# Cross attention and value experts in one block, with the first tiles of x1 normalised beside the last batch

## The reference

```
x = x + tanh(g_xattn) * cross_attention(layernorm(x), ctx)     # 16 heads of 16
x = x + tanh(g_ffn) * switchhead(layernorm(x))                 # 8 heads of 128
# switchhead(x), 8 value experts and 8 output experts for each head, top 2 of each:
gate_v, gate_o = top2(sigmoid(x @ sel_v.T)), top2(sigmoid(x @ sel_o.T))   # normalised
q, k = x @ q_w.T, x @ k_w.T
v    = sum_e gate_v[e] * (x @ v_w[e])
out  = sum_e gate_o[e] * softmax(q k.T / sqrt(128)) v @ o_w[e]
```

## Time and profile before

| | us |
|---|---|
| median of 3 runs | 1936.9 (1934.24 to 1937.22) |
| the profiled execution, by the clock of the runs | 1935.28 |
| its span in the profile | 1933.5 |
| TensorE busy | 1873.0 (97%) |
| VectorE busy | 1503.0 (78%) |
| ScalarE busy | 1137.4 (59%) |
| GpSimd busy | 935.6 (48%) |

### The profile page before, as it was taken

One profiled execution on the slowest core, in us unless ns is written; L12 is line 12 of the kernel. 1 busy time (PEld: TensorE's weight loads), 2 busy tenths in 40 slices (PEclk: granted clock), 3 DMA queues, 4 the chain that ended last, 5 costly groups with the idle time before them and its releaser, 6 DMA issues. The chain is left out here.

```text
span 1933.5 us, 57514 instructions
## 1 busy us (share of the span) xinstructions
PE 1873.0 (97%) x13454; PEld 1145.7 (59%) x13454; DVE 1503.0 (78%) x4285; ACT 1137.4 (59%) x3588; POOL 935.6 (48%) x1368
## 2 busy tenths in 40 slices
PE   5999999999997999999999999999999999999998
PEld 2678888888875555444444445545555555555553
DVE  6688888899887962555555556668999999999989
ACT  3678888888886444444444445545555555555543
POOL 4122222222212011666666666665776676776767
PEclk9999999999998999999999999999999999999999
DMA  3777888888871585000000023122222222222201
GB/s 124 144 117 118 119 120 120 119 119 120 119 98 55 214 330 208 27 27 20 21 27 27 27 67 105 55 66 72 71 80 66 80 74 70 80 67 79 75 13 66
DMA packets 192148, 174.22 MB, mean 90 GB/s; under 512 B 51921, under 2 KB 183378, under 8 KB 190034
## 3 DMA queue, kind: packets, MB, share of 16 engines
q1 hardware_dynamic: 189906, 165.06, 37.7%
q0 software_dynamic: 2176, 8.39, 1.2%
HBM read 112.41 MB, written 60.98 MB: 90 GB/s over the span
## 5 line engine op out<-in xcount | busy, mean ns | idle before, releaser
L1475 POOL TENSOR_TENSOR o_side<-o_side,o_tmp 128x256 f32 (+1 forms) x528 | 397.8, 753 | 194.7 <-POOL o_side L1475 72.3
L1244 PE MATMUL e_pv<-e_vw,e_xhi 128*128 (+1 forms) x1600 | 475.9, 379 | 1.2 <-ACT e_out L1167 1.2
L1177 ACT ACTIVATE big<-e_pv,gates 128x128 f32<-128x128 f32 x800 | 228.4, 369 | 280.2 <-PE e_pv L1244 278.6
L1603 ACT ACTIVATE o_tmp<-o_py,gates 128x256 f32<-128x256 f32 x528 | 222.4, 475 | 192.0 <-PE o_py L1675 138.6
L640 ACT ACTIVATE c_ex<-c_sm,c_nmax 100x361 f32<-100x361 f32 x512 | 302.6, 593 | 54.7 <-DVE c_nmax L523 49.7
L1675 PE MATMUL o_py<-o_whi,a_chi 128*128 128x512 f16 x800 | 304.3, 380 | 0.1
L1675 PE MATMUL o_py<-o_whi,a_clo 128*128 128x512 f16 x800 | 303.8, 380 | 0.0
L1675 PE MATMUL o_py<-o_wlo,a_chi 128*128 128x512 f16 x800 | 303.6, 379 | 0.0
L1244 PE MATMUL e_pv<-e_vw,e_xlo 128*128 (+1 forms) x800 | 303.2, 379 | 0.0
L523 DVE CUSTOM_DVE_ANT_0 c_sm<-c_ps,c_mbias 100x361 f32<-100x361 f32 x512 | 268.3, 525 | 38.9 <-PE c_ps L725 32.7
L1110 DVE TENSOR_SCALAR e_acc<-e_pv,gates 128x128 f32<-128x128 f32 x400 | 121.7, 346 | 218.6 <-PE e_pv L1244 218.5
(11 more groups left out here) (165 smaller groups left out, 3218.8 us busy)
## 6 DMA issues: line engine op xcount, KB each, us to landing
qk<-e_out SPq DMA_DIRECT2D x16, 1600.0 KB, 5.2
c_kst<-k_parts SPq DMA_DIRECT2D x256, 90.2 KB, 4.9
a_q<-qk SPq DMA_DIRECT2D x64, 200.0 KB, 2.4
a_k<-qk SPq DMA_DIRECT2D x64, 200.0 KB, 2.4
v<-e_out SPq DMA_DIRECT2D x20, 640.0 KB, 3.3
a_v<-v SPq DMA_DIRECT2D x64, 200.0 KB
c_ctx<-in_ctx_t SPq DMA_DIRECT2D x32, 361.0 KB, 3.4
e_wst<-in_v_w POOLq DMA_DIRECT2D x8, 1024.0 KB, 8.2
```

The lines of the kernel that those rows point to most:

```text
L1177: act.activation(tmp[:, hh, e, :], p_v[:, hh, 1, e * PD:(e + 1) * PD], ACT.Copy, scale=gate).then_inc(s_av, 1)
L1244: last = pe.matmul(p_v[:, hh, half, :], a[:, c, bass.ds(t * P, P)], vw[:, bass.ds(col + (w * DC + c) * VW, 512)], start=j == 0, stop=j == ...
L1475: pool.tensor_tensor(side[:, x.t, :], side[:, x.t, :], tmp[:, slot(x, r), j, :], ALU.add).then_inc(s_pool, 1)
L1603: act.activation(tmp[:, slot(x, r), j, :], p_y[:, q, j, :], ACT.Copy, scale=gate).then_inc(s_av, 1)
```

## The change

The two blocks become one (`layer`), so that the engines no longer meet at the border.

- The load of the selection weights is issued by SyncE (`sync_first`) after its last store of query parts and before `rest`. ScalarE's and VectorE's halves of their split (`scalar_first`, `vector_first`) stand after the queries and before `rest` on each engine.
- For the last batch, `rest` now ends, on VectorE, after the reciprocals, and on TensorE after turning them. Scaling (`tail(0)`), residual, moments and keeping (`tail(1)`) are called on VectorE among the experts' tiles 1 and 3; the projection is called on TensorE after the turn of tile 1.
- The root is taken in two parts: batches 0 to 29 before the first tile (`FIRST`), batches 30 and 31 (`REST`) at tile 4, on VectorE and on ScalarE.
- TensorE waits for the last residual before the second tile's logits, SyncE before the loads of route scale, query and key weights, GpSimd before the order constants.
- SyncE's wait for the stores of x1 is moved to behind the value stores.
- The selection weights and the root's tensors are placed elsewhere in SBUF.

```
 def rstd_steps(dve, mv, std, rstd, half, s_step, s_std, base):
-    dve.wait_ge(s_std, 1)
+    dve.wait_ge(s_std, base // 6 + 1)
...
# stage_cross, SyncE's rest
                 store(fixed(NB - 1))
-                for par in range(2):
-                    sp.wait_ge(s_st[par], 16 * NB // 2)
+        def sync_stored(sp):
+            for par in range(2):
+                sp.wait_ge(s_st[par], 16 * NB // 2)
...
# stage_cross, VectorE
                 rden_spread(last)
-                normalize(last)
-                residual(last)
-                moments(last)
-                mean_var(last)
-                keep(last)
+            def tail(n):
+                last = fixed(NB - 1)
+                if n == 0:
+                    normalize(last)
+                else:
+                    residual(last)
+                    moments(last)
+                    mean_var(last)
+                    keep(last)
+                    dve.wait_ge(s_kept, NB)
...
# stage_cross, TensorE
                 turn_rden(last)
-                for c in range(DC):
-                    project(last, c)
+            def tail():
+                project_all(fixed(NB - 1))
...
# stage_experts_in
+        def sync_first(sp):
+            sp.dma_start(sst[:, :, :], sel_t.rearrange("(c p) e -> p c e", p=P)).then_inc(s_sel, 16)
+        def vector_first(dve):
+            dve.wait_ge(s_whi, 1)
+            dve.scalar_tensor_tensor(out=slo[:, :, :], in0=sst[:, :, :], scalar=WS,
+                                     in1=shi[:, :, :], op0=ALU.mult,
+                                     op1=ALU.subtract).then_inc(s_wlo, 1)
+        def scalar_first(act):
+            act.wait_ge(s_sel, 16)
+            act.activation(shi[:, :, :], sst[:, :, :], ACT.Copy, scale=WS).then_inc(s_whi, 1)
         def sync(sp):
-            sp.dma_start(sst[:, :, :], sel_t.rearrange("(c p) e -> p c e", p=P)).then_inc(s_sel, 16)
+            sp.wait_ge(cross.s_x1, NB)
...
# GpSimd, among its normalisations
+                if b >= NB - 2:
+                    pool.wait_ge(s_step, 12)
                 normalize(pool, b).then_inc(s_xnp, 1)
+            pool.wait_ge(cross.s_x1, NB)
...
# VectorE
-            rstd_steps(dve, mv[0:SQ, :, :], std, rstd, half, s_step, s_std, 0)
+            def root(cut, base):
+                rstd_steps(dve, mv[0:SQ, cut, :], std[:, cut], rstd[:, cut], half[:, cut], s_step, s_std, base)
+            root(FIRST, 0)
...
                 if t >= 2:
                     x_lo(t - 2)
                 if t == 1:
-                    dve.wait_ge(s_whi, 1)
-                    dve.scalar_tensor_tensor(out=slo[:, :, :], in0=sst[:, :, :], scalar=WS,
-                                             in1=shi[:, :, :], op0=ALU.mult,
-                                             op1=ALU.subtract).then_inc(s_wlo, 1)
+                    tail(0)
+                if t == 3:
+                    tail(1)
+                if t == 4:
+                    root(REST, 6)
...
# ScalarE
+            root(FIRST, 0)
...
                 act.activation(xhi[:, :, tok], bank, ACT.Copy).then_inc(s_xhi, 1)
+                if t == 4:
+                    root(REST, 6)
...
# TensorE
+                if t == 1:
+                    pe.wait_ge(cross.s_x1, NB)
                 pe.wait_ge(s_xlo, -(-(t + 1) * P // SQ))
...
                 last.then_inc(s_t, 1)
+                if t == 1:
+                    tail()
                 for n in logit_tiles(t):
                     logits(n)
...
-def stage_experts(nc, e, o):
+def layer(nc, queries, cross, e, o):
     with nc.Block() as block:
         @block.sync
         def _(sp):
+            start, rest = cross.sync(sp)
+            queries.sync(sp, start)
+            e.sync_first(sp)
+            rest()
             e.sync(sp)
             o.sync_first(sp)
-            o.sync(sp, e.sync_values(sp))
+            store_values = e.sync_values(sp)
+            cross.sync_stored(sp)
+            o.sync(sp, store_values)
...
         @block.vector
         def _(dve):
-            o.vector(dve, e.vector(dve))
+            start, rest, tail = cross.vector(dve)
+            queries.vector(dve, start)
+            e.vector_first(dve)
+            rest()
+            o.vector(dve, e.vector(dve, tail))
         @block.scalar
         def _(act):
+            start, rest = cross.scalar(act)
+            queries.scalar(act, start)
+            e.scalar_first(act)
+            rest()
             o.scalar(act, e.scalar(act))
...
         @block.tensor
         def _(pe):
-            o.tensor(pe, e.tensor(pe))
+            start, rest, tail = cross.tensor(pe)
+            queries.tensor(pe, start)
+            rest()
+            o.tensor(pe, e.tensor(pe, tail))
```

More of the change, by code:

```diff
@@ L610, in rest @@
                 rden_spread(last)
-                normalize(last)
-                residual(last)
-                moments(last)
-                mean_var(last)
-                keep(last)
-            return start, rest
+            def tail(n):
[8 more added lines that the diff above has]
+                    dve.wait_ge(s_kept, NB)
+            return start, rest, tail
         def scalar_programs(act):
@@ L836, with stage_experts_in @@
     pass
-def stage_attention_in(nc, queries, cross):
-    with nc.Block() as block:
-        @block.sync
-        def _(sp):
-            start, rest = cross.sync(sp)
-            queries.sync(sp, start)
-            rest()
-        @block.gpsimd
-        def _(pool):
-            queries.gpsimd(pool)
-            cross.gpsimd(pool)
-        @block.vector
-        def _(dve):
-            start, rest = cross.vector(dve)
-            queries.vector(dve, start)
-            rest()
-        @block.scalar
-        def _(act):
-            start, rest = cross.scalar(act)
-            queries.scalar(act, start)
-            rest()
-        @block.tensor
-        def _(pe):
-            start, rest = cross.tensor(pe)
-            queries.tensor(pe, start)
-            rest()
-def stage_experts_in(nc, k, sems, big, mv, sel_t, q_t, k_t, v_t, rs, qk_out, v_out):
+def stage_experts_in(nc, k, sems, cross, big, mv, sel_t, q_t, k_t, v_t, rs, qk_out, v_out):
     with ExitStack() as ctx:
@@ L884, in stage_experts_in @@
         qkhi, qklo = (m.sbuf(f"e_qk{n}", [P, DC, 2 * H * PD], F16) for n in ("hi", "lo"))
-        sst = m.sbuf("e_sst", [P, DC, P])
-        shi, slo = (m.sbuf(f"e_s{n}", [P, DC, P], F16) for n in ("hi", "lo"))
-        std, rstd, half = (m.sbuf(n, [SQ, NB]) for n in ("e_std", "e_rstd", "e_half"))
         m1, m2, top, tot = (m.sbuf(f"e_{n}", [P, NT * 2 * H]) for n in ("m1", "m2", "top", "tot"))
@@ L903, in stage_experts_in @@
         tsum1 = m.sbuf("e_tsum1", [P, 2, PD])
+        sst = m.sbuf("e_sst", [P, DC, P])
+        shi, slo = (m.sbuf(f"e_s{n}", [P, DC, P], F16) for n in ("hi", "lo"))
+        std, rstd, half = (m.sbuf(n, [SQ, NB]) for n in ("e_std", "e_rstd", "e_half"))
+        FIRST, REST = slice(0, NB - 2), slice(NB - 2, NB)
         p_t = m.psum("e_pt", [P, 4, 512])
@@ L1135, in scalar, with root @@
         def scalar(act):
-            act.wait_ge(s_step, 1)
-            act.activation(std[:, :], mv[0:SQ, :, 1], ACT.Sqrt).then_inc(s_std, 1)
-            act.wait_ge(s_sel, 16)
-            act.activation(shi[:, :, :], sst[:, :, :], ACT.Copy, scale=WS).then_inc(s_whi, 1)
+            def root(cut, base):
+                act.wait_ge(s_step, base + 1)
+                act.activation(std[:, cut], mv[0:SQ, cut, 1], ACT.Sqrt).then_inc(s_std, 1)
+            root(FIRST, 0)
+            done = 0
             def probabilities(t):
@@ L1148, in scalar @@
                 act.activation(xhi[:, :, tok], bank, ACT.Copy).then_inc(s_xhi, 1)
-                for n in logit_tiles(t, lag=1):
-                    probabilities(n)
+                if t == 4:
+                    root(REST, 6)
+                if t >= 4:
+                    for n in range(done, logit_tiles(t, lag=1).stop):
+                        probabilities(n)
+                    done = logit_tiles(t, lag=1).stop
                 if t >= NB // 2 and t % 2 == 0:
@@ L1189, in scalar, with tensor @@
             return last_pair
-        def tensor(pe):
+        def tensor(pe, tail):
             def logits(t):
@@ L1712, in _ @@
         def _(sp):
+            start, rest = cross.sync(sp)
+            queries.sync(sp, start)
+            e.sync_first(sp)
+            rest()
             e.sync(sp)
             o.sync_first(sp)
-            o.sync(sp, e.sync_values(sp))
+            store_values = e.sync_values(sp)
+            cross.sync_stored(sp)
+            o.sync(sp, store_values)
         @block.gpsimd
         def _(pool):
+            queries.gpsimd(pool)
+            cross.gpsimd(pool)
             o.gpsimd(pool, e.gpsimd(pool))
@@ L1777, in flamingo @@
             mv = m.sbuf("x1_mv", [P, NB, 2])
-            with ExitStack() as innermost, ExitStack() as sems:
+            with ExitStack() as innermost:
                 c = cross_inputs(nc, innermost)
```

(5 more changed lines are left out.)

6 lines of the change are left out of this document (4 added, 2 removed).

## The result

The changed kernel takes **1949.83 us** (median of 6 runs, 1946.49 to 1954.53) against 1937.06 for the kernel before (6 runs of the same session, 1934.24 to 1941.26). The ratio is 1.0067 with a 95% interval of 1.0054 to 1.008: 12.8 us slower. The forecast was 1947.3 with a range of 1940 to 1951. The profiled execution of the changed kernel took 1948.39 us (span 1946.6), 13.1 more than the one before.

The account below looks back on a forecast made before the run. TensorE was taken to pace the cross attention (busy 511.45 of 520 us) and the query/key projection. Start 9.85 + clock 2.0 - border 1.4 = 10.4 us on 1935.28, plus 1.6 for the median: 1947.3, range 1940 to 1951.

Parts of the forecast that it names:

- The wait at the start: Cross attention's start: splits wait for the selection weights' load behind the query stores; first masked scores 9.85 us late.
- the early landing of that rival: Cross attention's start: the load overtakes the stores, start only 5.3 us late, total 1942.3; chance 0.14.
- Nothing made up for later: Cross attention's later batches: none of the start's delay is recovered, with batch 2's query wait of 1.4 us as bound.
- the larger catching up of that rival: Cross attention: batches 1 to 3 take up the 9.85 us, only the border is left, 1935.5 to 1931.5; chance 0.05.
- The clock at the start: Cross attention's start: TensorE works at half clock after its pause, costing 2.0 us, bounds 0 to 3.
- The border, removed and put in the way: Border: normalisation 5.35 us earlier, last batch's steps and second root in the way, leaving -1.4 us; bounds -5.35, +1.2.
- if the clock is back: Experts' tiles after tile 5: VectorE's 0.6 us a tile unchanged at full clock; otherwise the 1.35 gain becomes a 1.2 loss.
- the rival of low clock at both ends: Start and border: clock costs 3 us at the start, border loses 1.2, sum 14, total 1950.9; chance 0.12.

Follow-up runs that it names:

- load early: Changed kernel, with SyncE issuing the selection weights' load before the first store of query parts, splits still at the start: 1939.58 us, ratio 1.0005.
- plain border: Changed kernel with that load issued early, last batch drained whole before one root over all 32 columns, no block end: 1937.84 us, ratio 0.9992.
- sigmoid ahead: Plain border with 21 unread identity matmuls, plus an unread two-column sigmoid on ScalarE right behind the root: 1934.63 us, ratio 0.9986.
- the kernel kept busy: Plain border plus 21 unread identity matmuls around the last projection, run twice: 1935.75 us (ratio 0.9992) and 1933.73 us (0.9979).
- the kernel repeated: The changed kernel unaltered, run again beside the second kernel with the load on GpSimd's queue: 1950.23 us, ratio 1.0062.

## Why the prediction was right

**The wait at the start** was right in mechanism and size. The issue came at 74.54 (forecast: not before 74.00), the landing took 7.3 us, the split started at 81.85 (81.4), the masked scores at 82.64 (82.35). The term was 9.85 and measured 10.15. Taking the upper end, by the full queue, was the right choice; the early landing of that rival did not occur, and the rule of the Trainium skill on completion out of order (DMA: Bandwidth & Descriptors, Queues, rings and completion order) brought the load no earlier here. Whether the place in SyncE's queue or the traffic as a whole makes the 7.3 us is not shown: on GpSimd's queue, beside the same stores, a load took 7.5 and 7.7. That this wait is the loss is shown twice, by moving the split alone and the load alone.

**Nothing made up for later** was near enough. I had written that the wait for batch 2's queries "shifts too". That 1.4 us wait is absent from the waits of the changed kernel between 85 and 125 us, and the delay falls from 10.69 to 9.44 between batches 0 and 1. But this is no catching up during the pause: the wait is also absent in three kernels that have no pause (load early, plain border, sigmoid ahead), and it was 1.3 us in one profile of the kernel kept busy and 0.5 in the other. It differs from execution to execution. From batch 4 to batch 27 the delay stays at 9.8 to 10.1 (9.8 to 10.3 up to batch 14 in the kernel repeated), so the larger catching up of that rival did not occur.

**The clock at the start** was the term that was mis-sized: 2.0 forecast, and nothing that these traces can tell from zero. The heads of batch 0 are 0.54 us later than the first masked scores are (10.69 less 10.15), which is less than that distance varies without any low clock, and from batch 4 on the delay is no larger than that of the first masked scores. The low stretch is there, but some 6.6 us of its 10.2 lie over the pause. I had let it begin with the work.

**The border, removed and put in the way**, was right step by step up to the second root: first normalisation 3.18 us behind the copy (3.22 forecast), the second root 1.95 us from its addition to the next normalisation (1.9). Then the steps came out shorter than forecast, with the residual 0.44 us earlier, and tile 5's remainder started at 12.20 (13.05). The table load of 1.28 us follows the copy of 0.34 us without a gap, as in the earlier trace rows, and the drain that the Trainium skill (ScalarE: Activation LUTs, What ACT_TABLE_LOAD costs) adds is not seen. So 2.20 us were gained at tile 5 where 1.35 was forecast, but only 0.58 stood at the first query/key matmul: the forecast let VectorE's pace be unchanged "if the clock is back", and the clock was not back. The gain is still 1.93 at tile 8's remainder and 0.74 at tile 11's. In just that stretch the clock was low here, until about 619.4, 15.8 us behind the copy, where it was back 14.4 behind it before, and VectorE waited 0.61 and 0.25 us for ScalarE's copies, which waited for TensorE's transposes. That the clock is the cause is argued from this, not shown. It is a part of what the rival of low clock at both ends had described.

**What the sum did not have** is the clock behind the border. The first query/key matmul starts after a wait of 2.17 us for VectorE; before, the wait was 2.08 us and the clock stayed at 1.00, here it fell to 0.50 at 636.4 and came back at 639.8, and the first value matmul came 1.67 us later for it (132.95 us behind instead of 131.28). Every kernel with an interleaved border shows 132.6 to 133.7 there, with a low stretch of 3.4 us or more at the first query/key matmuls each time, and the plain ones without the sigmoid 131.3, with none. The plain border with the sigmoid ahead has the stretch too (132.99), so an interleaved border is not needed for it. About 1.1 us more came behind the last value matmul (11.7 us late); the clock had a low stretch of 6.8 us at 1319 there, which was 3.4 at 1310 before.

So the terms came out as 9.9 for the start with its clock (11.85 forecast), 0.6 for a low clock in the last batches (585 to 589, none forecast), -0.58 for the border (-1.4), +1.67 and +1.1 behind it (none), and 0.3 at the end: 13.0 of 13.1. The forecast's 10.4 was near partly by luck: an overrated clock at the start stood in for an overlooked one later. Part of these small terms is the execution's and not the change's: the profile of the same kernel repeated had its copy at 606.21 instead of 603.54.

**That the border gives nothing back** held for every order that was tried: no version of the interleaved border was faster than the kernel before by more than 0.2%. What the removed block end is worth is shown by the plain border: 2.1 us at the root, from the engines' meeting and the table load that moves beside the drain, not from normalising early. The 2.6 us at the first query/key matmul contain the clock's part as well. The best version found is the plain border with the early load and TensorE kept busy. Its second set of runs is 0.21% faster than the kernel before, its first 0.08%, so it is about 0.15% faster; one of the two intervals reaches 1.0001. That is 3 us, and no more than the spread of single runs. Adding the sigmoid gives the same within the intervals.

## What to carry to other kernels

A load that is moved to an earlier stage should be placed ahead of the large transfers of that stage, or its user should not stand in an engine's queue ahead of the stage's own work: either one alone took away the loss here, though neither made a gain. Before two stages are interleaved, ask which engine carries both: where it is the same one, as VectorE here, the early start is paid for within the same stage, and all that was had here is the fixed cost beside it, the table load and the engines' meeting. Differences of 3 us between single profiles say little in a kernel like this one: two profiles of the same kernel differed by as much, and the medians of two sets of 12 runs of the same kernel, from two sessions, by 2 us.

## What was not expected of the hardware

- **The clock falls after short pauses, and not each time.** A wait of 2.08 us before the first query/key matmul left it at 1.00 in the kernel before, and one of 2.17 us was followed by 0.50 in the changed one. The length does not decide it: the same kernel repeated waited 2.08 us and fell, and the plain border waited 2.16 and did not. At the border of the plain version it fell within 594 to 595, where the pauses of TensorE just ahead were of 0.60 us (at 592.07) and 0.89 us (at 594.00).
- **Matmuls nobody needs hold it at one place and only move the fall at another.** Some 5 us of them at the border kept it at 1.00 there in four profiles; 48 at the start moved the low stretch from 76 to 87 us and made it 3.4 us long instead of 10.2.
- **A 128 KB load takes 2.9 us with nothing else under way, 7.2 to 8.7 behind stores of 400 KB on SyncE's queue, and 7.5 to 7.7 on GpSimd's queue beside those stores.** The other queue made it no shorter. In these runs the data came much earlier only where the load was issued earlier.
- **The spread of this kernel's runs, some 4 us to each side, goes with low stretches of 3.4 to 13.7 us** that appear at different places in each profile (mostly within 72 to 91, 575 to 644, 1289 to 1330). In each set of ten runs or more the longer runs have the lower mean clock (correlations of -0.3 to -0.85). What decides where they come was not found.
